# A macaron of six sublayers on one core: the mixture of eight with resident biases, six weight buffers and transpositions two tiles ahead

## What is computed

```python
x = x + 0.5 * mixture_of_eight(layernorm(x))
x = x + softmax_attention(layernorm(x))
x = x + 0.5 * mixture_of_eight(layernorm(x))
x = x + 0.5 * mixture_of_sixteen(layernorm(x))
x = x + linear_attention(layernorm(x))
x = x + 0.5 * mixture_of_sixteen(layernorm(x))
```

```python
h = gelu(einsum('td,edp->etp', xf, W1) + b1[:, None, :])     # 128 -> 512
y = einsum('etp,epd->etd', h, W2) + b2[:, None, :]           # 512 -> 128
out = einsum('te,etd->td', router_weights, y)
```

## Time and profile before

| what | us |
|---|---|
| median of 3 runs | 1465.75 |
| lowest, highest | 1464.15, 1467.71 |
| the profiled execution, its own time | 1466.02 |
| its span in the profile | 1464.2 |
| PE busy | 1181.2 (81%) |
| DVE, ACT, POOL busy | 851.7, 749.7, 694.8 |
| first mixture of eight: outputs of tile 0 and tile 70 (L2200) | 74.1, 267.8 |
| second mixture of eight: outputs of tile 0 and tile 70 | 756.1, 939.7 |

### The profile page before, as it was taken

How to read it: one execution, slowest core, us unless ns; L and a number is a source line. 1 busy time by engine, 2 the same in 40 slices (tenths; PEclk the granted TensorE clock), 3 DMA queues, 4 the chain that set the end, 5 groups by cost and what they waited for, 6 DMA issues and landing times.

```text
span 1464.2 us, 26404 instructions
## 1 busy us (share of the span) xinstructions
PE 1181.2 (81%) x7620; PEld 795.6 (54%) x7620; DVE 851.7 (58%) x2897; ACT 749.7 (51%) x1707; POOL 694.8 (47%) x933
## 2 busy tenths in 40 slices
PE   4387788699999999999859889618999777479994
PEld 3377678322232322322349888616889665358894
DVE  7521356688988999989542466742124687622125
ACT  4244344167677677677735555413344666433441
POOL 3774325122234444443663357672554357634553
PEclk9999999789999999999979999858999978589997
DMA  6377877744354453343147778624558231145586
GB/s 200 106 200 222 252 214 207 221 138 138 99 164 130 113 143 105 101 141 100 48 111 201 209 205 239 191 85 135 178 176 258 87 110 44 47 125 172 169 262 200
DMA packets 197147, 228.56 MB, mean 156 GB/s; under 512 B 27312, under 2 KB 146480, under 8 KB 197008
## 3 DMA queue, kind: packets, MB, share of 16 engines
q1 hardware_dynamic: 165328, 183.32, 44.3%
q0 software_dynamic: 17856, 36.74, 7.2%
q10 hardware_dynamic: 13824, 6.82, 1.6%
HBM read 156.77 MB, written 69.76 MB: 155 GB/s over the span
## 4 chain that ended last, share of the span: by engine, by line
PE 47%; DVE 19%; DMA 10%; POOL 7%; SPq 6%; issue 6%; ACT 5%; DVEq 0%; POOLq 0%; ACTq 0%
PE PS L1463 14%; PE PS L1473 13%; DVE arena L2388 6%; DMA arena<-experts 6%; POOL dispatched L795 5%; PE PS L1650 5%; PE PS L1626 4%; ACT arena L1176 2%; PE PS L1441 2%; DVE X L1936 2%; PE PS L1634 2%; DVE BST L1926 2%; PE PS L1612 1%; DMA qk_products<-arena 1%; DMA YC<-expert_out 1%
## 5 line engine op out<-in xcount | busy, mean ns | idle before, releaser
L1052 ACT ACTIVATE arena<-PS,arena 128x128 f32<-128x128 f32 (+2 forms) x824 | 296.5, 419 | 401.5 <-PE PS L1463 392.9
L817 POOL DMA_INDIRECT expert_out<-arena x302 | 290.7, 963 | 346.7 <-issue 155.3
L1176 ACT ACTIVATE arena<-PS 128x512 f32<-128x512 f32 x512 | 283.9, 597 | 134.8 <-PE PS L1626 134.0
L1463 PE MATMUL PS<-arena 128*128 128x128 f32 (+2 forms) x1648 | 319.1, 339 | 41.2 <-DMA arena<-experts 39.9
L2388 DVE TENSOR_REDUCE arena<-PS 128x2 f32<-128x1024 f32 x256 | 300.8, 1216 | 31.5 <-PE PS L1636 30.6
L1473 PE MATMUL PS<-arena 128*128 128x128 f32 (+1 forms) x2416 | 311.0, 278 | 4.9 <-DVE arena L2200 3.9
L1473 PEld LDWEIGHTS PS<-arena 128*128 128x128 f32 x2416 | 297.5, 195 | 17.9 <-issue 8.1
L2200 DVE TENSOR_TENSOR arena<-PS,arena 128x128 f32<-128x128 f32 (+2 forms) x206 | 72.7, 353 | 392.4 <-PE PS L1473 390.8
L1463 PEld LDWEIGHTS PS<-arena 128*128 128x128 f32 x1648 | 241.1, 200 | 84.1 <-DMA arena<-experts 50.4
L795 POOL DMA_INDIRECT dispatched<-arena x192 | 185.7, 967 | 80.1 <-issue 58.2
L1626 PE MATMUL PS<-arena 96*128 96x512 bf16 x512 | 173.7, 391 | 12.1 <-ACT arena L1176 5.4
(11 more groups left out here) (273 smaller groups left out, 1186.8 us busy)
## 6 DMA issues: line engine op xcount, KB each, us to landing
arena<-experts SPq DMA_DIRECT2D x158, 256.0 KB, 5.0
arena<-experts SPq DMA_DIRECT2D x64, 578.0 KB
qk_products<-arena SPq DMA_DIRECT2D x48, 384.0 KB, 4.4
arena<-qk_products SPq DMA_DIRECT2D x64, 288.0 KB
YC<-expert_out SPq DMA_DIRECT2D x48, 256.0 KB
dispatched<-FILL SPq DMA_DIRECT2D x32, 322.5 KB, 3.4
arena<-experts SPq DMA_DIRECT2D x142, 66.0 KB
arena<-dispatched SPq DMA_DIRECT2D x142, 64.5 KB
```

Of the source, the lines that this page charges most:

```text
L817: pool.indirect_dma_start(YK, bass.IndirectOffsetOnAxis(ap=ID[:, s:s + 1], axis=0), YS[:, s, :], None).then_inc(s_yo[r], 16)
L1052: act.activation(HT[:, tau % PAIR, q, 0:S * P], hidden_chunk(S, q), func, bias=biases(f, tau)[:, q:q + 1]).then_inc(s_g, 1)
L1176: act.activation(PT[:, G % 2, j, k, :], bank(4 + k % 2), ACT.Exp, scale=float(1.0 / np.sqrt(HD))).then_inc(s_exp, 1)
L1463: pe.matmul(hidden_chunk(size(f, tau), q), ups(f, tau)[:, q * P:q * P + P], XPT[:, tau % PAIR, 0:N], start=True, stop=True).then_inc(s_h, 1)
```

## The change

- The biases of an expert stay on the chip beside its second weights: a resident is 644 columns in place of 512, and the load of biases for each tile is gone. ACT and DVE must then find the expert's biases by a register that they load for every tile.
- The ring of ups has six buffers, those of XPT and of the gelu's output four, for the mixtures of eight.
- PE turns tiles two ahead (`lead_of` is 2), and DVE copies as far ahead.
- SP loads rows and ups of one tile together; it clears one tail behind each of the tiles 8 to 11, and waits for s_tiles once, behind tile 8.
- Smaller moves: the statistics of a gathered group one step later; the even gates of the first mixture at step 8; the exponentials of the gates ahead of ACT's own clears; the residents' eighth expert in the second mixture loaded later in the attention. The third mixture's buffer is cleared between tiles 25 and 40 as it was.

```diff
-UP, DOWN, NARROW = FC * P, FC * D, FC + D
+UP, DOWN = FC * P, FC * D
+STAY = DOWN + FC + D
...
+UPS = 6
+DEEP = 4
...
+        def ring_of(f):
+            return UPS if moe_of(f)["E"] == E0 else RING
+        def lead_of(f):
+            return DEEP - 2 if moe_of(f)["E"] == E0 else 1
+        def halves(f):
+            return DEEP if moe_of(f)["E"] == E0 else PAIR
...
             def expert_stays(f, e):
                 at = PLACES[first_kind(f)][e]
-                sp.dma_start(arena[:, at:at + DOWN], ex0_in[e, :, UP:UP + DOWN]).then_inc(s_stay, 16)
+                sp.dma_start(arena[:, at:at + STAY], ex0_in[e, :, UP:WROW]).then_inc(s_stay, 16)
...
                 def rows_in(tau):
...
-                        sp.dma_start(biases(f, tau), ex0_in[bass.ds(found[tau], 1), :, UP + DOWN:WROW]
-                                     .rearrange("o p n -> p (o n)")).then_inc(s_rows[r], 16)
...
-                def follow(tau, rows=True):
-                    sp.wait_ge(s_h, (T0 + tau - (RING - 1)) * FC)
-                    ups_in(tau)
-                    if rows:
-                        sp.wait_ge(s_yc, T0 + tau - RING)
-                        rows_in(tau + XRING - RING - 1)
...
+                    if tau >= XRING:
+                        sp.wait_ge(s_yc, T0 + tau - (XRING - 1))
+                    sp.dma_start(XP[:, r, 0, :], BUFS[0][bass.ds(row, P), :]).then_inc(s_rows[r], 16)
+                    if tau >= UPS:
+                        sp.wait_ge(s_h, (T0 + tau - (UPS - 1)) * FC)
+                    sp.dma_start(ups(f, tau), ex0_in[bass.ds(row // REGION, 1), :, 0:UP].rearrange("o p n -> p (o n)"))\
+                      .then_inc(s_we[tau % UPS], 16)
...
-                clear_tails()
-                for tau in range(RING, soon - lead):
-                    follow(tau)
+                for tau in range(soon):
+                    rows_in(tau)
+                    if tau == XRING:
+                        sp.wait_ge(s_tiles, k + 1)
+                    if 0 <= tau - XRING < E0 // 2:
+                        clear_tail(tau - XRING)
...
             def tile_gelus(f, tau):
+                if moe_of(f)["E"] == E0:
+                    stay = act.value_load(stay_of(tau, early_of(f)), min_val=0, max_val=ARENA - STAY)
                 for q in range(FC):
+                    if moe_of(f)["E"] == E0:
+                        bias = arena[:, bass.ds(stay + (DOWN + q), 1)]
...
                 hidden(begin(L))
                 find(begin(L) + 1)
                 for c in range(begin(L) + 1, last_step(L) + 1 if carries(L) else tiles + 1):
-                    if c + 1 < tiles:
-                        turn(c + 1)
+                    if c + lead < tiles:
+                        turn(c + lead)
...
             def outputs_out(f, tau):
+                if moe_of(f)["E"] == E0:
+                    stay = dve.value_load(stay_of(tau, early_of(f)), min_val=0, max_val=ARENA - STAY)
+                    bias = arena[:, bass.ds(stay + (DOWN + FC), D)]
...
                         for b in early_starting(L, c):
                             gather(f, b, 1)
+                        for b in early_starting(L, c - 1):
                             group_stats(b * GT).then_inc(s_st1, 1)
```

More of the change, by code:

```diff
@@ L264, in build @@
         NMT = cv([8 * GT], BF16)
+        assert cv.at == TURNED_AT
         OT = cv([SEQ])
@@ L319, in build @@
         s_slot, s_disp = sem("slots_ready"), sem("rows_dispatched")
-        s_we = [sem(f"expert_in{r}") for r in range(RING)]
+        s_we = [sem(f"expert_in{r}") for r in range(UPS)]
         s_stay = sem("experts_in")
@@ L383, in expert_loads, with turned, bent @@
         def expert_loads(f, tau):
[L385 to L393, removed]
+            r = tau % ring_of(f)
+            before = sum(len(range(r, moe_of(j)["tiles"], ring_of(j))) for j in range(f) if r < ring_of(j))
+            return before + tau // ring_of(f) + 1
+        def ring_of(f):
[4 more added lines that the diff above has]
+            return DEEP if moe_of(f)["E"] == E0 else PAIR
+        def turned(f, tau, n):
+            return XPT0[:, tau % DEEP, 0:n] if moe_of(f)["E"] == E0 else XPT[:, tau % PAIR, 0:n]
+        def bent(f, tau):
+            return HT0[:, tau % DEEP] if moe_of(f)["E"] == E0 else HT[:, tau % PAIR]
         def stay_of(tau, soon):
@@ L409, in ups, with early_of, row_loads @@
                 return WE[:, tau % RING, 0:UP]
-            return arena[:, RING_AT + UP * (tau % RING):RING_AT + UP * (tau % RING + 1)]
+            return arena[:, RING_AT + UP * (tau % UPS):RING_AT + UP * (tau % UPS + 1)]
+        def early_of(f):
+            return BEGUN if first_kind(f) else SOON
+        def row_loads(f, tau):
+            before = sum(len(range(tau % XRING, moe_of(j)["tiles"], XRING)) for j in range(f))
+            return (tau % XRING < XCHUNKS) + before + tau // XRING + 1
         def scattered0(f, r):
@@ L635, in ups_in @@
[L635 to L650 removed]
+                    r = tau % XRING
@@ L676, in eight @@
                     sp.wait_ge(s_cleared, CLEARED - 16 * E1)
-                for tau in range(soon - lead, tiles):
-                    follow(tau)
+                for tau in range(soon, tiles):
+                    rows_in(tau)
                     if f == 0 and 0 <= tau - soon < E1:
@@ L1564, in moe @@
                 find(begin(L))
-                turn(begin(L))
-                turn(begin(L) + 1)
+                lead = lead_of(f)
+                for tau in range(begin(L), begin(L) + lead + 1):
+                    turn(tau)
                 hidden(begin(L))
@@ L2234, in moe @@
                     score_gap(f)
-                if E == E0 and not under_attention(L):
-                    even_gates(f)
-                elif E == E1:
+                if E == E1:
                     gates = shares(f)
@@ L2500, in attention @@
                 rows_turned(f, 1)
-                for part in range(2):
-                    choose(NG - 1, part)
+                choose(NG - 1, 0)
+                rows_turned(f, 2)
+                choose(NG - 1, 1)
                 score_gap(f)
```

124 lines of the change are left out of this document (66 added, 58 removed).

## The result

The changed kernel takes **1442.55 us** (median of 4 runs, 1438.99 to 1445.41), the kernel before 1466.73 in the 4 runs beside it (1464.15 to 1467.82). The ratio is 0.9836, with a 95% interval of 0.9805 to 0.9868: faster by 24 us, where 40 were forecast. The profiled execution took 1439.94 us, its span 1438.1.

The account below looks back on a forecast made before the run. PE was taken as the floor at 1.99 us a tile, with most stretches above it, mainly waiting for ups behind SP's issuing. Terms -5 -6 -13 -4 -6 -5 -1 gave -40, from 1466 to 1426 us; range 1408 to 1454.

Parts of the forecast that it names:

- the register loads: ACT and DVE, one load each per tile, 142 times: counted at nothing; if uncovered, up to 0.55 us a tile.
- The second rival: Register loads bind where DVE has most to do: 0.55 us in 37 tiles, 20 us, whole 1446 us; chance 0.14.
- the last 34 tiles: End of the second mixture: -1 us, no wait for ups standing out; bounds +6 and -5.
- tiles 42 to 70: First mixture's last stretch: -4 us, less than half of PE's 10.1 us of copy waits; bounds +5 and -10.
- tiles 4 to 24: First mixture: -6 us, 42.0 for 48.0, as SP without the bias slot falls below PE's 1.99 us a tile.
- the second mixture's start: Its first 11 tiles: -6 us, ups of tile 4 no longer waiting for s_tiles; bounds -3 and -9.
- its tiles 12 to 36: Second mixture: -5 us, most of the 6.0 us of waits for ups going; bounds -2 and -10.
- Tiles 25 to 41: First mixture, beside the clears: -13 us, 44 for 57.1, with DMA engines driven at 0.93; bounds -5 and -18.
- the first rival: DMA engines bound the tiles among the clears: -5 us there in place of -13, whole 1434 us; chance 0.20.
- The start: First mixture's start: 7 us gained, 2 paid for a third turn and the gelu table load, net -5.
- The fourth rival: Six buffers stay unfilled because SP stands in waits for scattered outputs: gain 32 us, whole 1434 us; chance 0.10.
- The slower rival: Every tile's loop grows, ACT and DVE waiting in register instructions: gain eaten from 0.28 us a tile, 1504 at 0.55; chance 0.10.

## Why the prediction was right in its direction and too high in its gain

**The step that failed is the one on the register loads, counted at nothing.** They cost 24.5 us on DVE. The prediction argued with DVE's busy share over the last stretch, 54.0 of 83.1 us. That is an average over steps of two kinds: in full steps DVE works without a pause and PE waits for it, and there the loads add 0.3 to 0.8 us a step, 11.5 us in 20 steps with the step behind each group of them; the 14 light steps together are no longer than without loads (29.6 us for 30.2). The evidence stood in the earlier trace rows: PE's eight waits for the copy meant that DVE was already last in eight of 34 steps. The cover named for ACT was real by the 4.8 us of its loads, for DVE it wasn't. The second rival, chance 0.14, named this mechanism and priced it at 20 us from 0.55 a load in 37 tiles. Its price of a load was about right, 11.5 us in 20 steps are 0.58 each, and so was its total, 1446 for a result of 1442.55 (the forecast: 1426). Its places were not: in the last 34 tiles 20 steps paid in place of 8, in tiles 42 to 70 the loads cost 5.1 us in place of 16, and another 7.8 lay in tiles 4 to 24 and 12 to 36, where it had none. So its total is in part luck.

The floor of about 600 ns that the Trainium skill gives a register load (DMA: Bandwidth & Descriptors, section Latency and other measured facts) was set aside for the 307 ns row of PE. DVE's load itself takes 311 ns, so the row was right for the instruction. But its register instructions follow, and from the load's start to L2224's the median of the 142 tiles is 0.64 us in the changed kernel's trace, near the Trainium skill's figure; in the step shown above DVE was idle for 0.79.

**Point by point.** Without DVE's loads the terms come out within about 1 us of the forecast or better: tiles 4 to 24 in 42.2 us (42.0 forecast), tiles 42 to 70 in 69.5 (71.7), the second mixture's start in 26.9 (26.4), its tiles 12 to 36 in 60.8 (63.2), its last 34 in 83.2 (82.1), the whole 48.7 us faster than before in place of 40. Tiles 25 to 41 took 41.7, below the 44 forecast, at a share of 0.87, not the 0.93 assumed: 268 x 41.7 = 11.2 MB were moved in the stretch where 13.65 - 1.15 = 12.5 had been reckoned, so part of its loads already lay ahead of it, and the first rival (the DMA engines bind at 0.80) falls. Tile 24 came 9.2 us earlier against tile 0 (51.7 for 60.9), where 13 had been named as a sign; without DVE's loads it is 12.9. The start paid 2.7 us for 2. Its 7 us were taken from a whole stretch, and so held the 1.8 us of the low clock without naming it. ACT's clears did end the second start. The fourth rival falls by the trace: until the last rows of a mixture are issued, none of SP's waits for scattered outputs is over 0.4 us, and the waits for ups are 0.9 in all. That tiles 42 to 70 won only 1.1 us, near that rival's 0, is the loads' doing.

**Whether the sum's parts add.** The prediction gave the tails' place 7 us and SP's bias slot 6 us of their own. To tile 24 the runs show that they hang together: with the bias DMA back, the tails' new place saves nothing that the totals show (61.3 for 60.9). Over the whole it stays open. Either run, with the DMA back or with four buffers, is as slow as the kernel before, but that does not make the other parts worth nothing, since both carry DVE's loads, 24.5 us, and the kernel before has none. Their prices, 27 and 23, stand against the 48.7 us that the change gains without those loads, and the second holds the late outputs as well.

**The slower rival** had its mechanism, a growth in every tile, at 0.28 us or more. The growth was 0.17 a tile on average, nearly half of it in the last 34 tiles and there in DVE's full steps.

## What to carry to other kernels

A load into a register cost little here on an engine that waits for others ahead of it, and about its whole length on one that is behind; so look at the engine's idle time just ahead of the place, step by step, not at its share. If steps come in full and light ones, load ahead in the light ones, and leave alone the step in which the engine catches up. Where a queue works in order, a ring's depth also sets when everything behind it in the queue starts, so an experiment on the depth moves those loads too. And hold the price of a part against the gain without the change's own losses, not against what is left of it.

## What the hardware showed that was not expected

An instruction of DVE that needs no register still waits for the loads ahead of it in the program: three loads left it idle for 1.62 us, one for 0.79 behind other DVE work, and in none of the 142 tiles did L2224 start before its load and register instructions were through. The same number of loads cost 4.8 us by the medians on ACT and 24.5 on DVE. A 66 KB transfer a tile that nobody reads, but that SP issues and PE's turn waits for, cost 26.6 us over 142 tiles, 0.19 us each, though PE, DVE and the clears did the same work. A stall of 5.11 us cost PE 6.9, since its next tile ran at a granted clock of 0.50.
